# A decoder layer whose keys and values come from one product of 512 columns instead of two of 256

## The reference, cut to what matters

```python
x = x + attn(layernorm(x))        # linear attention, 16 heads of 16
x = x + xattn(ctx, ctx, masks, layernorm(x))
x = x + ffn(layernorm(x))         # Hadamard, gate/up 256 -> 1024, silu, Hadamard, down

def attn(h):
    q, k, v = heads(h @ q_w.T + q_b), heads(h @ k_w.T + k_b), heads(h @ v_w.T + v_b)
    qp, kp = elu(q) + 1, elu(k) + 1
    kv = einsum('bhsd,bhse->bhde', kp, v)
    z = einsum('bhsd,bhd->bhs', qp, kp.sum(axis=2))[..., None]
    return merge(einsum('bhsd,bhde->bhse', qp, kv) / (z + 1e-6)) @ o_w.T + o_b

def xattn(q, k, masks, score):    # score = layernorm(x), 256 x 256 per batch
    return softmax(mask(((q @ Wq + bq) @ (k @ Wk + bk).T) / 8 * score))
```

## Time and profile before

| | |
|---|---|
| timed runs | 125.69 us median (125.47 to 125.76) |
| the profiled execution, its own time | 125.14 us |
| its span, first to last instruction | 123.3 us |
| TensorE (PE) | 119.2 us busy, 97%, 804 matmuls |
| VectorE (DVE) | 82.7 us, 67%, 207 instructions |
| ScalarE (ACT) | 71.6 us, 58%, 158 |
| GpSimd (POOL) | 68.5 us, 56%, 89 |
| chain of waits that ended last | PE 97% of it |
| L1177 (K and V) | 96 matmuls of 256 columns, 14.0 us, 288 ns each |

### The profile page before, as it was taken

One profiled execution on the slowest core, in us unless ns is written; L12 is line 12 of the kernel. 1 busy time (PEld: TensorE's weight loads), 2 busy tenths in 40 slices (PEclk: granted clock), 3 DMA queues, 4 the chain that ended last, 5 costly groups with the idle time before them and its releaser, 6 DMA issues.

```text
span 123.3 us, 2272 instructions
## 1 busy us (share of the span) xinstructions
PE 119.2 (97%) x804; PEld 107.0 (87%) x804; DVE 82.7 (67%) x207; ACT 71.6 (58%) x158; POOL 68.5 (56%) x89
## 2 busy tenths in 40 slices
PE   5999999999999999999999999999999999999990
PEld 2259999999999999999989999988888888889890
DVE  1399989899889899899998959674522332220521
ACT  1785696679748689888491479983135444280000
POOL 2228959979979966959802605762005574066000
DMA  3999910280000000000000110000110000000121
GB/s 123 316 377 423 398 76 5 53 330 3 8 0 0 0 5 3 0 0 0 0 5 0 43 45 0 5 0 0 39 46 3 5 0 0 0 0 0 54 73 43
DMA packets 3823, 7.64 MB, mean 62 GB/s; under 512 B 544, under 2 KB 1952, under 8 KB 3684
## 3 DMA queue, kind: packets, MB, share of 16 engines
q1 hardware_dynamic: 3806, 7.50, 16.8%
q10 hardware_dynamic: 6, 0.01, 0.0%
HBM read 6.46 MB, written 1.05 MB: 61 GB/s over the span
## 4 chain that ended last, share of the span: by engine, by line
PE 97%; POOL 0%; DVE 0%; issue 0%; POOLq 0%
PE bank L1283 19%; PE bank L1295 18%; PE bank L1300 11%; PE bank L1177 10%; PE bank L1304 5%; PE bank L1201 5%; PE bank L1239 5%; PE bank L1155 4%; PE bank L1115 4%; PE bank L1211 3%; PE bank L1221 3%; PE bank L1309 2%; PE bank L1146 2%; PE bank L1247 2%; PE bank L1128 1%; PE bank L1259 1%
## 5 line engine op out<-in xcount | busy, mean ns | idle before, releaser
L1283 PE MATMUL bank<-xh_home,wug 128*128 128x256 f32 x192 | 24.7, 285 | 0.0
L1283 PEld LDWEIGHTS bank<-xh_home,wug 128*128 128x128 f32 x192 | 23.6, 191 | 0.1
L1295 PE MATMUL bank<-xh_home,wug 128*128 128x512 f32 x96 | 22.0, 390 | 0.0
L1295 PEld LDWEIGHTS bank<-xh_home,wug 128*128 128x128 f32 x96 | 18.0, 188 | 3.7
L969 DVE SCALAR_TENSOR_TENSOR back<-bank,sc_up,back 128x512 f32<-128x512 f32 x8 | 6.0, 751 | 15.0 <-PE bank L1295 15.0
L351 POOL TENSOR_TENSOR hs<-back,hs 128x256 fp32r<-128x256 f32 x8 | 5.9, 740 | 17.0 <-ACT hs L614 16.9
L345 POOL TENSOR_TENSOR hs<-front,hs 128x256 fp32r<-128x256 f32 x16 | 11.5, 740 | 6.6 <-ACT hs L599 6.6
L1177 PE MATMUL bank<-watt,xT 128*128 128x256 f32 x96 | 14.0, 288 | 0.0
L1177 PEld LDWEIGHTS bank<-watt,xT 128*128 128x128 f32 x96 | 12.3, 189 | 0.9 <-ACT xT L492 0.7
L606 ACT ACTIVATE back<-bank,vecs 128x512 f32<-128x512 f32 x8 | 5.5, 688 | 12.1 <-PE bank L1295 12.1
L1300 PE MATMUL bank<-wdh,hs 128*128 128x512 f32 x48 | 12.5, 396 | 0.0
(11 more groups left out here) (132 smaller groups left out, 257.6 us busy)
## 6 DMA issues: line engine op xcount, KB each, us to landing
wd_a<-in_w_d SPq DMA_DIRECT2D x1, 1024.0 KB, 8.0
front<-in_w_ug SPq DMA_DIRECT2D x2, 512.0 KB, 8.5
back<-in_w_ug SPq DMA_DIRECT2D x2, 512.0 KB, 3.8
out<-x_res SPq DMA_DIRECT2D x8, 128.0 KB, 1.9
wd_b<-in_w_qkv SPq DMA_DIRECT2D x3, 256.0 KB, 4.5
x_res<-in_x SPq DMA_DIRECT2D x1, 512.0 KB, 6.0
x_res<-in_x_first SPq DMA_DIRECT2D x1, 385.0 KB, 3.1
back<-in_ctx_t SPq DMA_DIRECT2D x1, 260.0 KB
```

The lines of the kernel that those rows point to most:

```text
L1283: ins = mm(dst[:, n * SEQ:(n + 1) * SEQ], wug[:, wa, k, at_col + j * P:at_col + (j + 1) * P], xh[b][:, xb, k, :], start=(i == 0), stop=(i ...
L1295: ins = mm(dst[:, :].rearrange("p (b s) -> p b s", s=SEQ), wug[:, wa, k, at_col + j * P:at_col + (j + 1) * P], xh_home[:, PAIR, cols], sta ...
```

## The change

K and V of a batch become one step, `KV`. For each block of 128 positions six matmuls with the same stationary operand produce 512 columns, 256 of K and 256 of V, in one bank; a seventh of 256 columns adds K's bias to the left half. The two blocks of a batch fill two neighbouring banks, so `exp_k`, `elu_k` and `v_add` each read 256 columns of both banks in one instruction, and each waits for both banks. In `HEAD` `KV` stands where `K` stood, for batches 0 to 2; for batch 3 `XH 0`, which stood between `K 3` and `V 3`, now comes ahead of `KV 3`. The bank counts stay: one K and one V bank before, two KV banks after. A KV bank is free for its next group when `v_add` has read it. On VectorE `v_add(2)` moves from behind `at_lo(1)` to behind `softmax(0)`. Cut to its core:

```diff
-HEAD = (("mx", 0), ("u", 0), ("T1", 0), ("u", 1), ("K", 0), ("V", 0), ("Q", 0), ("T1", 1), ("SC", 0),
-        ("ST", 0), ("K", 1), ("NUM", 0), ("V", 1), ("T1", 2), ("AT", 0), ("Q", 1), ("OUT", 0), ("ST", 1),
-        ("K", 2), ("NUM", 1), ("V", 2), ("SC", 2), ("T1", 3), ("SC", 3), ("AT", 1), ("Q", 2), ("OUT", 1),
-        ("ST", 2), ("SC", 1), ("T3", 0), ("K", 3), ("XH", 0), ("V", 3), ("Q", 3), ("NUM", 2), ("ST", 3),)
+HEAD = (("mx", 0), ("u", 0), ("T1", 0), ("u", 1), ("KV", 0), ("Q", 0), ("T1", 1), ("SC", 0),
+        ("ST", 0), ("KV", 1), ("NUM", 0), ("T1", 2), ("AT", 0), ("Q", 1), ("OUT", 0), ("ST", 1),
+        ("KV", 2), ("NUM", 1), ("SC", 2), ("T1", 3), ("SC", 3), ("AT", 1), ("Q", 2), ("OUT", 1),
+        ("ST", 2), ("SC", 1), ("T3", 0), ("XH", 0), ("KV", 3), ("Q", 3), ("NUM", 2), ("ST", 3),)
...
+        before[group], last[b] = last.get(b), group
...
+        def both(i, c):
+            first_bank = bank_of["KV", i, 0]
+            assert bank_of["KV", i, 1] == first_bank + 1
+            return psum[:, first_bank:first_bank + 2, c * HID:(c + 1) * HID]
...
+            if name == "KV":
+                eng.wait_ge(s["vx"], i + 1)
...
-                wait_full(act, "K", b)
+                for i in range(ST):
+                    wait_full(act, "KV", b, i)
...
-                a.activation(ek[:, :], B("K", b)[:, :], ACT.Exp, bias=neg1[:, :]).then_inc(s["ek"], 1)
+                a.activation(ek[:, :].rearrange("p (i d) -> p i d", i=ST), both(b, 0), ACT.Exp, bias=neg1[:, :]).then_inc(s["ek"], 1)
...
             softmax(0)
+            v_add(2)
             ln_stats(3, 0)
             at_lo(1)
-            v_add(2)
...
-                if turn_of[name, i, t]:
-                    pe.wait_ge(read_of(name, i, t), turn_of[name, i, t])
+                if before[name, i, t]:
+                    wait_read(pe, *before[name, i, t])
...
-            def kv_proj(name, b, c):
-                dst = take(name, b)
+            def kv_proj(b):
                 pe.wait_ge(s["xT_hi"], b + 1)
                 if b == 0:
...
+                    pe.wait_ge(s["w_hi"], 2)
+                for i in range(ST):
+                    dst = take("KV", b, i)
                     for n, (k, wa, xb) in enumerate(X_PASSES):
                         if b == 0 and i == 0 and wa:
...
+                            pe.wait_ge(s["w_lo0"], 1)
+                            pe.wait_ge(s["w_lo1"], 1)
                         if i == 0 and xb:
                             wait_read(pe, "T1", b)
...
+                        mm(dst.rearrange("p (c o) -> p c o", c=2), xT[:, b % 2, xb, k, i * P:(i + 1) * P],
+                           wqkv[:, wa, 0:2, k, :], start=(n == 0), stop=(n == len(X_PASSES) - 1))
...
+                    done(mm(dst[:, 0:HID], ones[:, 0:P], bias_r[:, K_COLS], start=False, stop=True, skip_group_check=True), "KV", b, i)
...
             def state(b):
-                wait_read(pe, "K", b)
-                wait_read(pe, "V", b)
+                pe.wait_ge(s["kp"], b + 1)
+                wait_read(pe, "KV", b)
```

More of the change, by code:

```diff
@@ L76, in banks_of @@
 def banks_of(group, i):
-    return [(group, i, t) for t in range(2)] if group in ("NUM", "Y", "GG") else [(group, i, 0)]
+    return [(group, i, t) for t in range(2)] if group in ("NUM", "Y", "GG", "KV") else [(group, i, 0)]
 def schedule():
@@ L97, in decoder_kernel @@
 def decoder_kernel(nc, x_first, x, ctx_t, w_qkv, bias, w_o, w_ug, w_d, vec, row, row_wsd, mask, const, out):
-    bank_of, turn_of = {}, {}
+    bank_of, turn_of, reads_before, before = {}, {}, {}, {}
+    last, reads = {}, [0] * BANKS
     for n, group in enumerate(schedule()):
-        bank_of[group], turn_of[group] = n % (BANKS - 1), n // (BANKS - 1)
+        b = n % (BANKS - 1)
+        bank_of[group], turn_of[group] = b, n // (BANKS - 1)
+        before[group], last[b] = last.get(b), group
+        reads_before[group] = reads[b]
+        reads[b] += group[0] != "KV"
     for b in range(ST):
-        bank_of["SC", b, 0], turn_of["SC", b, 0] = BANKS - 1, b
+        bank_of["SC", b, 0], turn_of["SC", b, 0], reads_before["SC", b, 0] = BANKS - 1, b, b
     stack = ExitStack()
@@ L202, in decoder_kernel @@
         masks = bytes_of[:, TILES * SEQ:(TILES + BATCH + ST) * SEQ]
-        bank = [stack.enter_context(nc.psum_tensor(f"bank{i}", [P, 512], F32)) for i in range(BANKS)]
+        psum = stack.enter_context(nc.psum_tensor("bank", [P, BANKS, 512], F32))
+        bank = [psum[:, i, :] for i in range(BANKS)]
         full = [sem(f"bank_full{i}") for i in range(BANKS)]
@@ L219, in wait_read @@
         def wait_read(eng, name, i, t=0):
-            eng.wait_ge(read[bank_of[name, i, t]], turn_of[name, i, t] + 1)
+            if name == "KV":
+                eng.wait_ge(s["vx"], i + 1)
+            else:
+                eng.wait_ge(read[bank_of[name, i, t]], reads_before[name, i, t] + 1)
         loads = "x0 x1 x2 cst wk wv wq ctx bias vec row wsd mask wo wd ug0 ug1 ug2 ug3".split()
@@ L229, in decoder_kernel @@
                  "ug_hi ug_lo fly pre_hi pre_lo wd wd_hi "
-                 "xT_hi ek eq z_eps z_inv at_hi "
+                 "xT_hi ek kp vx eq z_eps z_inv at_hi "
                  "sx logit prob rsum x2 "
@@ L498, in exp_k @@
             def exp_k(b):
-                wait_full(act, "K", b)
+                for i in range(ST):
+                    wait_full(act, "KV", b, i)
                 if b:
-                    wait_read(act, "K", b - 1)
-                a.activation(ek[:, :], B("K", b)[:, :], ACT.Exp, bias=neg1[:, :]).then_inc(s["ek"], 1)
+                    act.wait_ge(s["kp"], b)
+                a.activation(ek[:, :].rearrange("p (i d) -> p i d", i=ST), both(b, 0), ACT.Exp, bias=neg1[:, :]).then_inc(s["ek"], 1)
             def exp_q(b):
@@ L550, in mix_in @@
                 else:
-                    wait_read(act, "K", BATCH - 1)
+                    act.wait_ge(s["kp"], BATCH)
                 a.activation(mix[:, 0, :], B("T3", b)[:, 0:SEQ], ACT.Copy, scale=vecs[:, V_SUG:V_SUG + 1]).then_inc(s["mix_in"], 1)
@@ L803, in elu_k @@
                     wait_full(dve, "ST", b - 2)
-                v.scalar_tensor_tensor(kp[:, b % 2, :, :].rearrange("p i d -> p (i d)"), ek[:, :], 1.0, B("K", b)[:, :],
-                                       ALU.min, ALU.max).then_inc(read_of("K", b), 1)
+                v.scalar_tensor_tensor(kp[:, b % 2, :, :], ek[:, :].rearrange("p (i d) -> p i d", i=ST), 1.0, both(b, 0),
+                                       ALU.min, ALU.max).then_inc(s["kp"], 1)
             def v_add(b):
-                wait_full(dve, "V", b)
+                for i in range(ST):
+                    wait_full(dve, "KV", b, i)
                 if b == 0:
@@ L815, in v_add @@
                 v.tensor_tensor(vx[:, b % 2, :, 0:P].rearrange("p (i g) e -> p i g e", i=ST),
-                                B("V", b)[:, :].rearrange("p (i g e) -> p i g e", i=ST, g=FB),
+                                both(b, 1).rearrange("p i (g e) -> p i g e", g=FB),
                                 rows[:, 1:2, :].rearrange("p i (g e) -> p i g e", g=FB).to_broadcast([P, ST, FB, P]),
-                                ALU.add).then_inc(read_of("V", b), 1)
+                                ALU.add).then_inc(s["vx"], 1)
             def elu_q(b):
@@ L1163, in turn3 @@
                 turn("T3", b, xn3)
-            def kv_proj(name, b, c):
-                dst = take(name, b)
+            def kv_proj(b):
                 pe.wait_ge(s["xT_hi"], b + 1)
                 if b == 0:
-                    pe.wait_ge(s["w_hi"], c + 1)
+                    pe.wait_ge(s["w_hi"], 2)
                 for i in range(ST):
-                    into = dst[:, i * HID:(i + 1) * HID]
+                    dst = take("KV", b, i)
                     for n, (k, wa, xb) in enumerate(X_PASSES):
                         if b == 0 and i == 0 and wa:
-                            pe.wait_ge(s[f"w_lo{c}"], 1)
+                            pe.wait_ge(s["w_lo0"], 1)
+                            pe.wait_ge(s["w_lo1"], 1)
                         if i == 0 and xb:
                             wait_read(pe, "T1", b)
[L1177 to L1190, removed]
+                        mm(dst.rearrange("p (c o) -> p c o", c=2), xT[:, b % 2, xb, k, i * P:(i + 1) * P],
+                           wqkv[:, wa, 0:2, k, :], start=(n == 0), stop=(n == len(X_PASSES) - 1))
+                    if b == 0 and i == 0:
+                        pe.wait_ge(s["bias"], 1)
+                        pe.wait_ge(s["ones"], 1)
+                    done(mm(dst[:, 0:HID], ones[:, 0:P], bias_r[:, K_COLS], start=False, stop=True, skip_group_check=True), "KV", b, i)
             def q_proj(b):
@@ L1372, in down_pair @@
                 done(ins, "Y", b, 1)
-            steps = {"mx": weights_product, "u": project, "T1": turn1, "SC": scores, "K": k_proj, "V": v_proj, "Q": q_proj,
+            steps = {"mx": weights_product, "u": project, "T1": turn1, "SC": scores, "KV": kv_proj, "Q": q_proj,
```

## The result

The changed kernel took 131.83 us (median; 130.81 to 135.67) beside 125.58 for the kernel before in the same rounds: a ratio of 1.0472, 95% interval 1.0369 to 1.0574. Some executions of several kernels, the kernel before (128.3 to 129.0 us) among them, lie some 3 us above the rest without a change in the mean clock; the medians take them in, the ratios leave them out. The profiled execution is of the first: 130.81 us, span 129.0, 5.7 longer than before.

The account below looks back on a forecast made before the run. TensorE's own time was taken as the bound. Shifts of 0.34 + 1.09 + 1.86 + 1.26 + 0.45 = 5.0 us on the profiled 125.14 give 130.1, plus 0.55 for the timed median 130.7 us; range 128.3 to 132.6.

Parts of the forecast that it names:

- What the products save: K and V products on TensorE: a pair goes from 238 to 227 ns, 48 pairs save 0.54 us (0.22 at 234).
- Batch 0: exp_k(0) waits for V too, so T1 1 ends at 14.30 instead of 13.96: +0.34 us (0.13 to 0.50).
- Batch 1: T1 2 waits for normalise(1,2), and AT 0 for attend(0), which V 1 covered before: +1.09 us more.
- Batch 2: AT 1 waits until v_add(2) has read a KV 2 bank, the largest pause, 2.1 us: +1.86 us more.
- Batch 3 and the first gate and up products: XH 0 waits for x3_hi(0) and x3_lo(0), +1.26 us more; first gate and up products for xh_lo(0), +0.45 more.
- (a): Waits grow less than summed as VectorE catches up during TensorE pauses; 128.8 us without AT 1's bank wait; 14%.
- (b): TensorE's own time stays the bound and the kernel gets faster, 124.6 us; 4%.
- (c): VectorE or GpSimd is late for a gate and up step between 44 and 62 us: 131.6 to 132.5 us; 13%.
- (d): The new pauses lower TensorE's clock, 1 to 5 us more between AT 1 and T3 0: some 133 us; 5%.
- (e): A 512-column product costs two of 256, so the merger saves nothing: 0.54 us more, inside the range; no chance given.

Follow-up runs that it names:

- experiment 5: The changed kernel with normalise(1,2) ahead of exp_k(1) in ScalarE's list: 131.37 us, ratio 1.0462 to the kernel before.
- experiment 2: The changed kernel with v_add(2) ahead of softmax(0) in VectorE's list: 130.02 us, ratio 1.038 to the kernel before.
- experiment 3: The changed kernel with KV 3 ahead of XH 0, where K 3 stood: 128.97 us, ratio 1.0307 to the kernel before.
- experiment 1: The changed kernel with each 512-column product taken apart into two of 256, same order, banks and waits: 132.31 us, ratio 1.0551 to the kernel before.
- experiment 4: The kernel before with the new order alone; K and V keep own products and banks, exp_k waits for K alone: 129.77 us, ratio 1.034.
- experiment 7: The changed kernel with steps reordered on TensorE, ScalarE and VectorE to cover every pause, ctx_lo(1) ahead of attend(0): 130.42 us, ratio 1.0318 to the kernel before.
- experiment 8: The kernel of experiment 7 with ctx_lo(1) back behind xT_lo(2) and elu_q(2) ahead of logits(1): 127.00 us, ratio 1.0128 to the kernel before.
- 9: The kernel of experiment 8 with wo_lo ahead of elu_q(0), both ctx_lo before GpSimd's long step, SC 2 between T1 2 and OUT 0: 125.91 us, ratio 1.0047.

## Why the prediction was right

Forecast 130.7 us, measured 131.83, within the range, in the direction and by the mechanism that were forecast.

The number came closer than its terms. The steps shift the profiled execution by 5.7 us where they were summed to 5.0, and the 0.55 added for timed runs above the profiled one did not come: the two executions at full clock lie at 130.81 and 131.01. So at full clock two errors nearly cancel, which is luck, and the median lies above them for the executions with the lower clock, which the sum did not hold.

- **What the products save**: 5 to 10 ns a pair by the rows above, against 11 taken and 5 as the other bound; KV takes 3.10, 3.08, 3.10 and 3.02 us. Right, at the lower half.
- **Batch 0** was mis-sized: +0.71 for +0.34, outside its bounds (0.13 to 0.50). KV 0 started 0.10 later, with the context's DMA, and took 3.10 us for 2.97; `exp_k(0)` began 0.27 behind TensorE's next step, not 0.20; so `normalise(1,1)` started at 13.25, not 12.9. That is half of the 0.72 us by which the first gate and up product came later than forecast; the other steps added 1.11, 1.96, 1.40 and 0.54 us where 1.09, 1.86, 1.26 and 0.45 were forecast, each forecast a little short.
- **Batch 1**: both waits came as described. The forecast counted them by the later one, attend(0); experiment 5 shows that this was right, since the other costs nothing without it.
- **Batch 2**: the bank wait, counted out from the order, was the largest pause, 1.85 us for 2.1 with its signal; experiment 2 shows that `v_add(2)` ends it and that `softmax(0)` ahead of it makes 0.98 of it.
- **Batch 3 and the first gate and up products**: shown by experiment 3, which takes these 1.8 us back with one place in the order.
- **The rivals.** (a) and (b) are out: the waits grew more than was added up, and the time rose. (c) did not occur: TensorE has no new pause behind 49.41 us. (d) occurs in some executions, and the median lies above the profiled execution for it: 5% was too little for a pause of 2 us, and it should have been an addition to the forecast, not a case of its own. (e) is out by experiment 1.

The Trainium skill, page "TensorE: Matmul & The Clock Gate", section "Why this matters for your kernels", names idle gaps as what brings the half clock back; the windows of experiment 1 agree that it can, with 0.50 behind 1.85 us of pause, while the changed kernel's profiled execution kept 1.00 behind the same pause.

## What to carry to other kernels

On an engine that is busy without a gap, a step's place pays as much as its length: taking V out from between dependent steps cost 4.4 us (experiment 4), and merging it with K saved 0.7 (experiment 1). Before two steps are merged, list for each what lies behind it and waits for it, and for each bank which reader frees it, in the new order; each place with less slack than the merged step's length becomes a pause, and they add up along the chain. Two waits at one place did not add in experiment 5: the later one alone counted.

## What the runs showed of the hardware that was not expected

In experiment 1 a pause of 1.85 us was followed by a lower clock for some 4 us of the timeline (0.63, 0.50, 0.50, 0.71), in some executions and not in others of the same kernel: 1.5 us more. Behind a pause of 1.49 us experiment 7 shows the same. Every execution with a mean clock under 0.99 is of a kernel with a pause of 1.49 us or more; where the longest behind the first products was 1.05 us or less (experiments 2, 4, 8 and 9) the mean stayed at 0.997 or above in all executions.

A VectorE subtraction with both inputs in SBUF and a long GpSimd step did not run together here. `ctx_lo(1)`, 65 x 512, took 0.68 us where it began first, in the kernel before, 1.66 in the changed kernel, 1.47 in experiment 8 and 2.87 in experiment 7, and in the last three it ended 0.54 to 0.55 us after GpSimd's step (25.36, 25.16 and 24.45). In the kernel before VectorE's began 0.04 earlier than GpSimd's, and GpSimd's step took 2.89 us instead of 2.4. The Trainium skill, page "SBUF — State Buffer", section "Who interferes with whom", says that such a VectorE instruction contends with GpSimd's reads and that the one issued first goes first; these rows agree.
